# Perceiver block on one core: another order of the work in the first four attention groups

## The reference, cut to what matters

```python
# block 1: cross attention, one head of 256
n = layernorm(x)
q, k, v = n @ Wq.T + bq, ctx @ Wk.T + bk, ctx @ Wv.T + bv
x = x + softmax(q @ k.T) @ v
# block 2: causal linear attention, 16 heads of 64, 128 features
n = layernorm(x)
q, k, v = n @ aWq, n @ aWk, n @ aWv          # 256 -> 1024
x = x + causal_linear(phi(q), phi(k), v) @ aWo
# block 3: feed-forward with quantised activations and weights
x = x + bitlinear(gelu(bitlinear(layernorm(x), w1)), w2)
```

## Time and profile before

| | before |
|---|---|
| median of 3 runs | 253.41 us |
| the profiled execution | 253.28 us |
| its span | 251.5 us |
| PE busy | 239.7 us, 95% of the span |
| DVE busy | 187.6 us, 75% |
| ACT busy | 146.5 us, 58% |
| POOL busy | 101.6 us, 40% |
| granted clock of TensorE | 9 tenths or more in each of the 40 slices |

### The profile page before, as it was taken

How to read it: one execution, slowest core, us unless ns; L and a number is a source line. 1 busy time by engine, 2 the same in 40 slices (tenths; PEclk the granted TensorE clock), 3 DMA queues, 4 the chain that set the end, 5 groups by cost and what they waited for, 6 DMA issues and landing times.

```text
span 251.5 us, 6988 instructions
## 1 busy us (share of the span) xinstructions
PE 239.7 (95%) x2722; PEld 188.8 (75%) x2728; DVE 187.6 (75%) x476; ACT 146.5 (58%) x284; POOL 101.6 (40%) x139
## 2 busy tenths in 40 slices
PE   7998889999999999999999999999999989999984
PEld 7854556777788778787777878777789978888863
DVE  5577888666742685777888888775688979999994
ACT  0554454534446888567656766765647257787772
POOL 2063113342202558344674578726720024444430
PEclk9999999999999999999999999999999999999999
DMA  7999999990079001100110000000000000000001
GB/s 189 357 390 404 398 395 393 344 390 33 1 252 330 4 0 46 44 3 1 44 44 3 1 3 3 3 0 3 4 3 3 4 0 3 21 23 21 22 26 63
DMA packets 15377, 26.83 MB, mean 107 GB/s; under 512 B 1232, under 2 KB 8688, under 8 KB 15344
## 3 DMA queue, kind: packets, MB, share of 16 engines
q1 hardware_dynamic: 14576, 25.96, 28.9%
q10 hardware_dynamic: 768, 0.43, 0.6%
HBM read 25.33 MB, written 1.05 MB: 105 GB/s over the span
## 4 chain that ended last, share of the span: by engine, by line
PE 63%; DVE 18%; issue 6%; POOL 5%; ACT 4%; DMA 2%; SPq 0%; DVEq 0%; POOLq 0%; ACTq 0%
PE b L1346 11%; PE b L1106 7%; PE b L1390 6%; PE b L1108 6%; PE b L1107 6%; PE b L1365 4%; PE b L1267 3%; PE b L1270 2%; PE b L1263 2%; DMA xwk<-in_xWk 2%; PE b L1520 2%; DVE yT_lo L980 2%; DVE xn L742 2%; PE b L1218 2%; PE b L1186 2%
## 5 line engine op out<-in xcount | busy, mean ns | idle before, releaser
L852 DVE TENSOR_TENSOR x_lo<-b,x_hi 128x512 fp32r<-128x512 f32 x32 | 21.7, 688 | 16.8 <-ACT x_hi L463 16.7
L600 ACT ACTIVATE phi<-b 128x512 f32<-128x512 f32 x48 | 26.0, 597 | 11.3 <-PE b L1346 11.3
L403 POOL TENSOR_TENSOR sq_lo<-sq_sum,sq_hi 128x512 fp32r<-128x512 f32 x16 | 20.6, 1287 | 25.8 <-ACT sq_hi L463 25.8
L345 POOL TENSOR_TENSOR lnr<-lnv,mh 128x1 f32<-128x1 f32 x16 | 8.8, 552 | 54.9 <-DVE lnv L716 54.7
L521 ACT ACTIVATE sq<-b 128x512 f32<-128x512 f32 x32 | 19.3, 603 | 18.1 <-PE b L1108 18.1
L397 POOL TENSOR_TENSOR sq_sum<-sq,sq 128x512 f32<-128x512 f32 x16 | 20.7, 1293 | 21.6 <-ACT sq L521 21.6
L1106 PE MATMUL b<-nT_lo,wp_hi 128*128 128x512 f32 x64 | 26.8, 418 | 0.1
L1108 PE MATMUL b<-nT_hi,wp_hi 128*128 128x512 f32 x64 | 25.0, 391 | 0.0
L1107 PE MATMUL b<-nT_hi,wp_lo 128*128 128x512 f32 x64 | 25.0, 390 | 0.0
L926 DVE TENSOR_TENSOR smk<-b,mask 64x512 f32<-64x512 f32 x32 | 22.0, 688 | 2.9 <-PE b L1365 1.2
L1390 PEld LDWEIGHTS b<-va,smk 128*64 128x64 f32 x512 | 17.5, 137 | 7.5 <-issue 7.1
(11 more groups left out here) (180 smaller groups left out, 615.9 us busy)
## 6 DMA issues: line engine op xcount, KB each, us to landing
cT<-in_ctxT SPq DMA_DIRECT2D x8, 1028.0 KB, 14.0
cn<-in_ctx SPq DMA_DIRECT2D x8, 1024.0 KB, 14.7
wv_raw<-in_aWv SPq DMA_DIRECT2D x1, 1024.0 KB, 13.8
wp_raw<-in_aWq SPq DMA_DIRECT2D x4, 256.0 KB, 4.0
wp_raw<-in_aWk SPq DMA_DIRECT2D x4, 256.0 KB, 4.2
w_raw<-in_w2T SPq DMA_DIRECT2D x1, 1024.0 KB, 5.4
wo<-in_aWo SPq DMA_DIRECT2D x1, 1024.0 KB, 7.9
w_raw<-in_w1T SPq DMA_DIRECT2D x1, 1024.0 KB, 5.0
```

What stands on the lines that cost most here:

```text
L403: nc.gpsimd.tensor_tensor(sq_lo[n % 2][:], sq_sum[:], sq_hi[n % 2][:].bitcast(F32), ALU.subtract).then_inc(sq_l, 1)
L600: nc.scalar.activation(phi(n, a)[:], feature_bank(a), ACT.Exp).then_inc(f_exp, 1)
L852: nc.vector.tensor_tensor(x_lo[n % 2][r][:], proj_bank(n, r), x_hi[n % 2][r][:].bitcast(F32), ALU.subtract).then_inc(x_l, 1)
```

## The change

It moves work of the first iterations, changes some loads and adds one small instruction:
- The two matmuls of the loop over c with bk (four in the profile) leave bias_v1 and stand in front of the m product. xwq's load has a semaphore of its own. On ACT's queue the order is now bk, xwq, bq, and behind them comes a copy of two columns into spare.
- x of groups 4 to 7 is loaded in two parts (4 and 5, 6 and 7), and wv_raw in two column halves, each with a semaphore of its own and at other places of SP's list. bvb's load moves from ACT's queue to SP's.
- stats(0,4,6) moves from iteration 0 to iteration 1, behind inverse_sum(1); the rest of the DVE's list in iterations 0 to 3 is in another order.
- In iteration 2 PE does avTt(1), xT(2), nT(0) and wv(1) ahead of scores(2).
- qk(2) moves from iteration 3 to 2, values(0,1) from 3 to 2, xT(3) from 4 to 3, qk(3) from 5 to 4. last_keys(3) moves behind pTt(1). t_bias(2) and t_bias(3) stay.
- add_bias(2) moves from before the loop into iteration 0 of POOL's loop.

```diff
@@ SP
             load_cT(1)
-            load_x(2, 4, NG)
+            sp.dma_start(bvb[:], bv.rearrange("(a d) -> a d", a=1).broadcast_to([P, D])).then_inc(ld_bv, 16)
+            load_x(2, 4, 6)
             load_cn(1)
+            load_wv(0)
             load_cT(2)
-            load_weight(wv_raw, aWv, ld_wv)
+            load_x(3, 6, NG)
+            load_wv(1)
             load_cn(2)
@@ POOL
-            for g in range(3):
+            for g in range(2):
                 add_bias(g)
             x_rstd(2)
...
                 if g == 0:
+                    add_bias(2)
                     add_bias(3)
@@ ACT
-            act.dma_start(xwq[:], xWq.rearrange("(c p) d -> p c d", p=P)).then_inc(ld_m, 16)
+            act.dma_start(bqk[:, 1, :], bk).then_inc(ld_bk, 16)
+            act.dma_start(xwq[:], xWq.rearrange("(c p) d -> p c d", p=P)).then_inc(ld_xwq, 16)
             act.dma_start(bqk[:, 0, :], bq).then_inc(ld_bq, 16)
-            act.dma_start(bqk[:, 1, :], bk).then_inc(ld_bk, 16)
+            act.wait_ge(setup_dve, 1)
+            copy(spare[:], mh[:, 0:2])
...
+                if i == 2:
+                    xT(2)
                 if 0 <= i - 2:
                     nT(i - 2)
...
-                if 0 <= i - 3:
+                if 1 <= i - 3:
                     vcopy(i - 3, 1)
-                if i == 0:
-                    clcopy(0)
-                if i == 1:
-                    clcopy(2)
                 if i < NG:
                     pTc(i)
+                if i < 2:
+                    clcopy(2 * i)
                 if i == 0:
                     xT(1)
-                    clcopy(1)
+                if i < 2:
+                    clcopy(2 * i + 1)
+                if i == 0:
                     qk(1)
-                if i == 1:
-                    clcopy(3)
-                if i == 3 or i == 5:
-                    qk((i + 1) // 2)
+                if i == 2:
+                    split_wv(1)
+                    qk(2)
+                if i == 3:
+                    xT(3)
+                if i == 4:
+                    qk(3)
                 if 0 <= i - 2:
                     vcopy(i - 2, 0)
                 if i == 2:
-                    split_wv(1)
-                if i == 2 or i == 4:
-                    xT((i + 2) // 2)
+                    vcopy(0, 1)
@@ DVE
                 if i == 2:
-                    avT(i - 1)
+                    avT(1)
+                    xT(2)
+                    nT(0)
                 if i < NG:
                     softmax_bias(i)
...
-                if i == 2:
-                    stats(0, 6, 8)
+                if i == 1:
+                    dve.wait_ge(ld_x[2], 16)
+                    stats(0, 4, 6)
                 if 0 <= i - 1:
                     settle()
                     x1(i - 1)
                     dve.wait_ge(x1_cp, i)
                     stats(1, i - 1, i)
+                if i == 2:
+                    dve.wait_ge(ld_x[3], 16)
+                    stats(0, 6, 8)
+                    split_wv_low(1, 0)
+                    split_wv_low(1, 1)
+                if i == 1 or i == 2:
+                    avc(i)
+                if i == 1:
+                    x_norm(4)
+                    x_norm(5)
+                if 0 <= i - 1:
                     x2_norm(i - 1)
+                if i == 2:
+                    x_norm(6)
+                    x_norm(7)
                 if i == 3 or i == 5:
                     t_bias((i + 1) // 2)
                 if i == 0:
                     xT(1)
-                if i < NG:
+                if i < NG and i != 1 and i != 2:
                     avc(i)
                 if i == 0:
                     t_bias(1)
-                    dve.wait_ge(ld_x[2], 16)
-                    stats(0, 4, 6)
-                if i == 1:
-                    x_norm(4)
-                    x_norm(5)
-                if i == 2:
-                    split_wv_low(1, 0)
-                    split_wv_low(1, 1)
-                if i == 2 or i == 4:
-                    xT((i + 2) // 2)
                 if i == 3:
-                    x_norm(6)
-                    x_norm(7)
+                    xT(3)
@@ PE
-            pe.wait_ge(ld_m, 32)
+            pe.wait_ge(ld_xwq, 16)
+            pe.wait_ge(ld_bk, 16)
+            for c in range(DC):
+                pe.matmul(b3[:, 0:D], bqk[:, 1, c:c + 1].broadcast_to([P, P]), xwq[:, c, :],
+                          start=(c == 0), stop=(c == DC - 1))
+            pe.wait_ge(ld_m, 16)
...
             for i in range(NG + 1):
+                if i == 2:
+                    avTt(1)
+                    xT(2)
+                    nT(0)
+                    wv(1)
                 if i < NG:
                     scores(i)
...
-                if 0 <= i - 3:
+                if 1 <= i - 3:
                     values(i - 3, 1)
-                if 0 <= i - 1:
+                if 0 <= i - 1 and i != 2:
                     wv(i - 1)
-                if i == 1:
-                    last_keys(3)
-                if i == 2 or i == 4:
-                    xT((i + 2) // 2)
-                if i == 3 or i == 5:
-                    qk((i + 1) // 2)
+                if i == 2:
+                    qk(2)
+                if i == 3:
+                    xT(3)
+                if i == 4:
+                    qk(3)
                 if i < NG:
                     pTt(i)
                 if i == 0:
                     xT(1)
+                if i == 1:
+                    last_keys(3)
                 if 0 <= i - 2:
                     values(i - 2, 0)
                 if i < NG:
                     avm(i)
                 if i == 0:
                     qk(1)
+                if i == 2:
+                    values(0, 1)
```

More of the change, by code:

```diff
@@ L206, in phi @@
             return phi_01[n % 2][a] if a < 2 else phi_23[n // 2 % 2][n % 2][a - 2]
-        ld_x = [sem(f"ld_x{i}") for i in range(3)]
+        ld_x = [sem(f"ld_x{i}") for i in range(4)]
         ld_cl, cl_zero, cl_sel, cl_mm, cl_cp = sem("ld_cl"), sem("cl_zero"), sem("cl_sel"), sem("cl_mm"), sem("cl_cp")
         ld_m, ld_bq, ld_bk, ld_ident, ld_bv = (sem(n) for n in ("ld_m", "ld_bq", "ld_bk", "ld_ident", "ld_bv"))
-        ld_c, ld_wv, ld_xwv, ld_w1, ld_w2, ld_mask, ld_wo = (
-            sem(n) for n in ("ld_consts", "ld_wv", "ld_xwv", "ld_w1", "ld_w2",
+        ld_c, ld_xwq, ld_xwv, ld_w1, ld_w2, ld_mask, ld_wo = (
+            sem(n) for n in ("ld_consts", "ld_xwq", "ld_xwv", "ld_w1", "ld_w2",
                              "ld_mask", "ld_wo"))
+        ld_wv = [sem(f"ld_wv{h}") for h in range(2)]
         ld_w = [sem(f"ld_aw{t}") for t in range(2)]
@@ L283, in load_weight, with load_wv @@
                 sp.dma_start(dst[:], w.rearrange("(c p) d -> p c d", p=P)).then_inc(done, 16)
+            def load_wv(hh):
+                cols = slice(HALF_E * hh, HALF_E * (hh + 1))
+                sp.dma_start(wv_raw[:, :, cols], aWv.rearrange("(c p) d -> p c d", p=P)[:, :, cols]
+                             ).then_inc(ld_wv[hh], 16)
             load_x(0, 0, 2)
@@ L532, in split_wv @@
             def split_wv(hh):
-                if hh == 0:
-                    act.wait_ge(ld_wv, 16)
+                act.wait_ge(ld_wv[hh], 16)
                 cols = slice(HALF_E * hh, HALF_E * (hh + 1))
                 copy(wv_hi[:, :, cols], wv_raw[:, :, cols]).then_inc(wv_h, 1)
-            act.dma_start(xwq[:], xWq.rearrange("(c p) d -> p c d", p=P)).then_inc(ld_m, 16)
+            act.dma_start(bqk[:, 1, :], bk).then_inc(ld_bk, 16)
+            act.dma_start(xwq[:], xWq.rearrange("(c p) d -> p c d", p=P)).then_inc(ld_xwq, 16)
             act.dma_start(bqk[:, 0, :], bq).then_inc(ld_bq, 16)
-            act.dma_start(bqk[:, 1, :], bk).then_inc(ld_bk, 16)
+            act.wait_ge(setup_dve, 1)
+            copy(spare[:], mh[:, 0:2])
             last = ctx[:, 2 * P, :].rearrange("(g b) d -> b g d", b=BG)
@@ L545, in _ @@
                 act.dma_start(clc[T * b:T * b + 1], last[b:b + 1]).then_inc(ld_cl, 16)
-            act.dma_start(bvb[:], bv.rearrange("(a d) -> a d", a=1).broadcast_to([P, D])).then_inc(ld_bv, 16)
             act.wait_ge(m_mm, 1)
@@ L871, in _ @@
                     avT(i - 1)
-                if 0 <= i - 2:
+                if 0 <= i - 2 and i != 2:
                     nT(i - 2)
@@ L1132, in bias_v1 @@
             def bias_v1():
-                pe.wait_ge(ld_bk, 16)
                 pe.wait_ge(ld_bq, 16)
-                for c in range(DC):
-                    pe.matmul(b3[:, 0:D], bqk[:, 1, c:c + 1].broadcast_to([P, P]), xwq[:, c, :],
-                              start=(c == 0), stop=(c == DC - 1))
                 for c in range(DC):
```

## The result

| | before | after |
|---|---|---|
| median of 20 runs | 253.44 us | 255.12 us |
| span of the profiled execution | 251.5 us | 253.4 us |
| PE busy | 239.7 us | 240.7 us |
| avTt(5) on PE | 56.73 us | 58.56 us |

The change makes the kernel slower: ratio 1.0058, 95% interval 1.0046 to 1.0071, about 1.5 us (the medians differ by 1.7). One of the 20 runs took 380.91 us at a granted clock of 0.56 and is left out of the ratio. Nearly all of the span's shift of 1.9 is there at avTt(5), the transposes of av of group 5: 1.83. What follows adds next to nothing, as the prediction assumed.

A forecast was written before the change was run, and what follows sets the result against it. PE's own work and the arrival of ctxT and ctx were the possible floors, with iterations 3 to 5 deciding by the DVE's queue. avTt(5) shifts by -0.3 + 0.96 = +0.7, giving 254.1 us; range with the others 252.8 to 255.1.

The forecast's parts named there:

- likeliest case: Whole kernel: avTt(5) 0.7 us later shifts the end one to one, 254.1 us, range 253.6 to 254.6, chance 0.50.
- my own bounds: Scores 3 up to 1.4 us earlier, -0.7; or start gains nothing (0.9 lost) and DVE conflict adds 0.7, +2.0 at most.
- Steps 5 and 6: Iterations 3 to 5: x1(2) at 36.9, avTt(3) 0.3 us earlier; qk(3) adds 0.96 in iteration 4, avTt(5) +0.7.
- the signs I named: Scores 2 near 26, scores 3 near 34, wv_lo wait over 1 us, idle about 1 before avTt(3), 1.5 to 1.7 before avTt(5).
- Step 1: Start: bk product before the m product; m product 0.3 us later, everything behind 0.5 earlier, of which 0.2 is carried.
- step 2: stats(0,4,6) behind inverse_sum(1) frees the DVE: softmax_bias(1) starts at 19.3 instead of 20.98, inverse_sum(1) at 20.8.
- step 3: Iteration 1 into 2: nT(0) waits for x2_norm(0) at 24.9; scores 2 at 26.0 to 26.1, the 1.7 us gained becomes 0.15.
- step 4: Iteration 2: 5.7 us of DVE work makes the last wv_lo ready at 32.9 to 33.0; scores 3 at 34.0, not 32.6.
- Rival 1: Iteration 2: no DVE backlog, last wv_lo ready by 31.6, scores 3 start when cT(3) lands at 32.6; 252.7 us, chance 0.17.
- Rival 2: A wash: DVE 0.6 to 0.8 us earlier, scores 3 at 33.3, qk(3) in iteration 4 takes it back; 253.4, chance 0.15.
- Rivals 3 and 4: Slower: Rival 3, or bk late or clc loads meeting last_keys(0), start losing 0.5 to 0.9 us, 254.7; together chance 0.18.
- Rival 3: Iteration 2: POOL's x_rstd(3), 0.70 us, falls beside split_wv_low(1,0); DVE waits, last wv_lo 0.7 later, 254.8.

The follow-up runs named there:

- c_vals_back: Changed kernel with values(0,1), its copy and the second pair of wv_lo splits put back where they were before: 254.20 us, ratio 1.0032 to the kernel before.
- b_tbias3: Changed kernel with t_bias(3) moved from before avc(5) in iteration 5 to behind avc(4) in iteration 4: 253.69 us, ratio 0.9996 to the kernel before.
- f_tb_after: Changed kernel with t_bias(2) moved behind avc(3) and t_bias(3) behind avc(4): 252.80 us, ratio 0.9967 to the kernel before.
- a_qk3_back: Changed kernel with qk(3) put back from iteration 4 to iteration 5: 253.79 us, ratio 1.0011 to the kernel before.
- k_bk_back: Changed kernel with the four bk matmuls back behind the m product, bk's load still first on ACT's queue: 255.17 us, ratio 1.0067 to the kernel before.
- n_more_cl: g_both plus x2_norm(1) before the second wv_lo pair, xT_lo(3) behind avT_lo(3), ACT's xT(1) before clcopy(0): 251.14 us, ratio 0.9908 to the kernel before.
- g_both: Changed kernel with the edits of f_tb_after and c_vals_back together: 252.05 us, ratio 0.9953 to the kernel before.

## Why the prediction was right, and where it was off

| | predicted | measured |
|---|---|---|
| softmax_bias(1) | 19.3 | 19.85 |
| scores 2 | 26.0 to 26.1 | 26.94 |
| last wv_lo | 32.9 to 33.0 | 33.90 |
| scores 3 | 34.0 | 35.07 |
| x1(2) | 36.9 | 38.05 |
| avTt(3) | 41.85 | 43.01 |
| avTt(5) | 57.4 | 58.56 |

- The direction is right, and the size is not: I said +0.7 (254.1), and it is +1.5 by the ratio, twice that. The measured 255.1 is above the likeliest case's own range (253.6 to 254.6) and at the upper end of the range with the others (255.1). That end doesn't follow from my own bounds either: 0.7, 0.9 and 0.7 make +2.3, where I wrote +2.0, and 255.1 is +1.7.
- Direction and mechanism are as forecast, in all three places: shown by c_vals_back (the DVE's row in iteration 2), b_tbias3 and f_tb_after (t_bias in front of av), a_qk3_back (qk(3) in iteration 4). Steps 5 and 6 hold to 0.1 each: x1(2), forecast 0.3 earlier than before, came 0.88 later because scores 3 were 1.07 later than I had them. Of the signs I named, the waits before avTt(3) (1.10) and avTt(5) (1.66) came; the wait for wv_lo was 0.85, not over 1, and scores 2 and 3 came 0.9 and 1.07 later than named.
- Step 1 failed. It took the 6.1 of xwk's landing over from the trace before, while the change reorders the two queues' first loads. The product delays the m product by as much as it saves behind it: 0.8 to 1.0 (6.40 to 6.53 in seven kernels with the product in front, 5.57 in k_bk_back) against 0.87 (7.83 to 8.70 in k_bk_back).
- In step 1, "xT_hi(1) gains 0.2 only" was still too much. It started at 16.11, against 16.04 before; n_more_cl shows 0.29 of clcopy(0)'s time in front of it. From scores 0 to scores 1 it is 6.46 to 6.49 us in the three kernels with the old order and in n_more_cl, and 6.69 to 6.73 in the eight others.
- In step 2, softmax_bias(1) was to start at 19.3 on the DVE's account alone. The DVE was free by then and waited 0.47 for scores 1, which at 18.63 were not earlier than before (18.64). That they end at 19.7 stood in the trace before, and I had left it out. It is 0.55 of the miss; some 0.35 of it is this execution's late start, for in k_bk_back, with the same loop, softmax_bias(1) starts at 19.48 after the same wait of 0.48.
- In step 3, avc(1) started 0.36 after the DVE was free, with avm(1)'s matmuls over at 23.75 by the profile. It is in all the kernels with this order (0.34 to 0.36 <- issue). What it waited for stays open. It is another 0.3 of the miss; 0.1 is the DVE's row in step 4, 5.82 for 5.7.
- The kernel moved by 1.5 to 1.7, not by the profile's 1.9. The profiled executions are not the median ones: 255.26 us is 0.14 above its median, 253.28 before is 0.16 below. The changed kernel's has the late start (scores 0 at 11.90): its bk product took 1.25 us from start to the m product, 0.97 in the seven others, and the profile doesn't show why.
- Rival 1, faster, did not come: its condition was the last wv_lo at 31.6, and it was ready at 33.90. Rival 2 had the DVE earlier than forecast; it was later. Rivals 3 and 4 are nearer in number (254.8, 254.7) than my forecast, but neither came as described. bk landed early enough and last_keys(0) did not wait for the clc loads; what was lost at the start is in the points above. Rival 3 did meet its place, with the other side as loser: x_rstd(3) on POOL became ready in the middle of the split and took 1.07 instead of 0.70, while the two splits kept their 1.29. It is 1.07 in the five kernels in which the split has just begun, and 0.70 in the seven others, here the changed kernel and c_vals_back:

```profile
32.79 1.07 POOL L342 TENSOR_TENSOR lnr<-lnv,mh 128x2 f32<-128x2 f32 x1 [0.59 <-DVE lnv L729]
...
32.33 0.70 POOL L342 TENSOR_TENSOR lnr<-lnv,mh 128x2 f32<-128x2 f32 x1 [0.59 <-DVE lnv L727]
```

The Trainium skill's page "SBUF — State Buffer", "SBUF: two separate sides", says that whichever starts first keeps the shared ports for its whole instruction and the other waits. The trace agrees: the split starts first, at 32.61, and POOL's instruction, at 32.79, takes 1.07 against 0.70. I had allowed 254.8 for the case in which the DVE is the one that waits. By the rule that needs POOL to start first. In c_vals_back and g_both it does, at 32.33 and 32.39, and the split starts at 32.59 and 32.65, before POOL's 0.70 us are over; it keeps its 1.28 and 1.29 all the same. POOL's spans are rough, so this says only that the forecast 0.7 us did not come in either order.

## What to carry to other kernels

When work of one engine is moved from one iteration to another, ask for both iterations which engine sets their length. Taken out where another engine is the bound, it gives nothing back; put in where its own engine is dense, it costs its full time. Here 1.4 us of qk(3) did both. A small step that hides behind that work, t_bias here, has to move with it, or behind the result that the next engine waits for. And a landing time read from the old trace is not a constant of the new one when the order of the loads is part of the change.

## What the runs showed of the hardware that I had not expected

- A t_bias of 1.9 to 2.1 us beside POOL's elementwise work takes 1.07 us when POOL is idle (0.42 and 0.42 for the two t_dot, 0.23 for the rest in b_tbias3, against 0.42 to 0.62, 0.94 or 0.95 and 0.56 in iterations 3 and 5 of the changed kernel). So it matters not only where a DVE step stands in the chain, but also what POOL does beside it.
- xwk, 256 KB, landed 3.8 to 4.0 us after its issue in the nine kernels in which xwq's load was issued second on the other queue, and 4.4 to 5.0 in the three in which it was first.
